# Row scatters of a routed expert layer: twelve in a row, or one at a time across the next step

## The chip, the cores and the metric

One core of one Trainium2 chip. The time is device microseconds for one execution of the whole kernel, median of three runs. All data is float32 except three small bf16 tiles.

## The reference

A transformer block with adaptive layer norm, for 8 images of 256 tokens and 256 channels:

```
mod = silu(c) @ wmod                       # 6 rows of 256 per image: sa, ca, ga, sb, cb, gb
h = layernorm(x) * (1 + ca) + sa
x = x + ga * attention(h)                  # 16 heads, ternary weights, chunks of 128 tokens with a carried state
h = layernorm(x) * (1 + cb) + sb
scores = sigmoid(h @ gate_w); best 4 of 8 groups, then best 6 of 64 experts
x = x + gb * (sum of 6 experts(h) + shared expert(h))
```

Each expert takes at most 48 tokens; the kernel keeps a table `rows_dram` with 64 slots for each of the 64 experts.

## The kernel before, in words

The kernel has three stages. **Token stage:** one step per image, `step(s, ...)` for s = 0 to 9 on every engine. Step s works on image s in attention (`cur`), on image s-1 in the output projection, residual and second norm (`has_prev`), and on image s-2 in the router's choice and the shared expert (`has_two`). **Expert stage:** 32 pairs of experts, `pair_step`; the token rows come back from DRAM (`rows_dram`), pass through the two experts and are scattered to `y_dram` by `put` (L489), one scatter a pair. **Last stage:** 16 tiles are read back, summed over their six experts (L1019), gated and stored.

Each engine has its own hand-written order of work in a step; counters (semaphores, `S[...]`) tie them together. `token_steps` (L257) calls the step for s = 0, 1, 2 as straight code, steps 3 to 6 as two turns of a hardware loop of two steps, and steps 7, 8, 9 as straight code again.

What the change and the prediction touch, in the order of one step:

- GpSimd's step (L454). `power` of `rstd1` for image s+1 (L456), `power` of `fac` for image s-1 (L458), `q_lam` (L463), `power` of `rstd2` for image s-1 (L465); then `h2s` (L469) and `h2row` (L473), the second norm's scale and shift; last `dispatch` (L441) of image s-2, twice six indirect DMAs (L449). Each writes 128 rows of `h2row` (336 floats) to the rows of `rows_dram` that `slot_ix` names.
- `h2row` and `slot_ix` have two buffers. GpSimd waits at L472 until the scatters of two images ago are written before it overwrites `h2row`.
- VectorE's step (L939): router scores of s-2 (L824), statistics of the first norm, shared expert, `out_norms` (L785: the row L790 waits for TensorE's L1120), `rms`, router choice (L840), mask 0 (L821), `state`, residual (L799, L805, L810) with the second norm's statistics (L654 to L662, whose last is `ve2`), first norm's output, second norm's output `z2` (L668), mask 1, `slots` (L919), which ends with `slot_ix`, and `shared_out`.
- TensorE's step (L1215): `project_qkv` (L1078 and on), scores, `project_out`, `values`, `norm2_transpose` (L1174, waits for `h2row`), logits (L1184), `norm1_transpose`, `gate_up` (L1193), and at the next step's head `out_stats` (L1120).
- ScalarE copies what TensorE leaves in PSUM: `qT`, `k_eo`, `v_eo`, `h2T`, `oT`, `r_exp`, `hT`, and `s_exp` (L614) after `gate_up`. `norm1_out` (L558) takes its scale and bias from `mod_cur`, which VectorE copies per image (L679).
- SyncE's queue loads `xa`, `mod_b` and `xres` in each step, and after the last step waits (L343) until all 96 row scatters are written; then it loads the rows for the experts (L346).

Of the kernel before, what the change touches and what calls it, by code (L numbers as in the profile page):

```python
# [5 lines left out]
ALU = mybir.AluOpType  # L6
# [7 lines left out]
P = 128  # L14
# [23 lines left out]
NBUF = 2  # L38
EPS_F = 1.1920928955078125e-07
# [23 lines left out]
def adaln_attention_moe(nc, x, qkv_w, qkv_norm_w, proj_w, proj_norm_w, norm_w, s, gate_w, bias,  # L63
                        w_gate, w_up, w_down, ws_gate, ws_up, ws_down, c, wmod, out):
    with ExitStack() as ctx:
# [58 lines left out]
        mod_cur = [sb(f"mod_cur{i}", [P, 4]) for i in range(2)]  # L124
# [22 lines left out]
        attn = sb("attn", [P, NT, C])  # L147
# [7 lines left out]
        h2row = [sb(f"h2row{i}", [P, NT, ROWW]) for i in range(2)]  # L155
# [24 lines left out]
        slot_ix = [sb(f"slot_ix{i}", [P, NT, 8], U32) for i in range(2)]  # L180
# [10 lines left out]
        wcol = [sb(f"wcol{i}", [P, 1]) for i in range(WBUF)]  # L191
        larger = sb("larger", [P, 8])
        rank = sb("rank", [P, 1])
        y_row = [sb(f"y_row{i}", [P, 1], U32) for i in range(WBUF)]

        spare = scm[:].rearrange("p r j q t -> p (r j q t)")
        row_bufs = [h[:] for h in h2row] + [spare[:, NT * ROWW * i:NT * ROWW * (i + 1)].rearrange("p (n c) -> p n c", n=NT)
                            for i in range(XBUF // 2 - 2)]
        xr = [row_bufs[i // 2][:, i % 2] for i in range(XBUF)]
        xt = [attn[:, i].rearrange("p (k r) -> p k r", k=KC) for i in range(NBUF)]  # L200
# [32 lines left out]
        ld_y2 ld_y3 ld_xr0 ld_xr1 ld_xr2 ld_xr3 st_mod st_zero st_rows0 st_rows1 st_put0 st_put1  # L233
        st_put2 st_put3 st_y0 st_y1 c_zero c_fill c_shape c_neg c_decay0 c_decay c_lam c_misc q_abs
        q_all q_tern q_tp q_sc q_w m_exp m_silu m_tp m_ct m_mm m_cols m_rows0 m_rows ln1_ve ln1_rstd
        z1_ready xt_done mod_cur_ready hT_ready hsq_ready q_done q_taken k_done k_taken v_done
# [20 lines left out]
        def token_steps(eng, step):  # L257

            for s in range(3):
                step(s, s % 2, s // 2, max(s - 1, 0) // 2)
            with eng.Fori(0, (B - 4) // 2) as i:
                step(2 * i + 3, 1, i + 1, i + 1)
                step(2 * i + 4, 0, i + 2, i + 1)
            step(B - 1, 1, (B - 1) // 2, (B - 2) // 2)
            step(B, 0, B // 2, (B - 1) // 2)
            step(B + 1, 1, (B + 1) // 2, B // 2)
# [26 lines left out]
        def _(sp):  # L295
# [44 lines left out]
            token_steps(sp, step)  # L340


            for par in range(2):  # L343
                sp.wait_ge(S[f"st_rows{par}"], 16 * B // 2 * NT * TOPK)
# [41 lines left out]
        def _(pool):  # L386
# [20 lines left out]
            for i in range(2):  # L407
                g.memset(h2row[i][:, :, TKEY:ROWW], 0.0)
# [32 lines left out]
            def dispatch(b, par, tile):  # L441

                if tile == 0:
                    pool.wait_ge(S["slots_ready"], b + 1)
                    pool.wait_ge(S["w_ready"], b + 1)
                    pool.wait_ge(S["h2_ready"], b + 1)
                    settle(par)
                for j in range(TOPK):
                    g.indirect_dma_start(  # L449
                        out=rows_dram, out_offset=bass.IndirectOffsetOnAxis(ap=slot_ix[par][:, tile, j:j + 1], axis=0),  # L450
                        in_=h2row[par][:, tile, :], in_offset=None, bounds_check=last_row,
                        oob_is_err=False).then_inc(S[f"st_rows{par}"], 16)

            def step(s, par, h, hp):  # L454
                if not at_end(s, B - 1):
                    power(rstd1[:], ve1[:], 0, "ln1_ve", "ln1_rstd", s + 2)  # L456
                if not before(s, 1) and not at_end(s, B + 1):
                    power(fac[:], fin[:, 4], 1, "f5", "f_ready", s)  # L458
                if not at_end(s, B):

                    pool.wait_ge(S["q_taken"], s + 1)
                    seen(pool, S["pv1"], s)
                    g.tensor_tensor(q_lam[:], qT[:, :, T:2 * T], lam_q[:], ALU.mult).then_inc(S["qlam_ready"], 1)  # L463
                if not before(s, 1) and not at_end(s, B + 1):
                    power(rstd2[:], ve2[:], 0, "ln2_ve", "ln2_rstd", s)  # L465

                    pool.wait_ge(S["z2_ready"], s)
                    pool.wait_ge(S[f"ld_modb{1 - par}"], 16 * (hp + 1))
                    g.tensor_tensor(h2s[:], z2[:], spread(mod_b[1 - par][:, 2], 1, NT), ALU.mult).then_inc(S["h2_mul"], 1)  # L469
                    pool.wait_ge(S["h2_mul"], s)  # L470
                    seen(pool, S["h2t_done"], s - 2)
                    seen(pool, S[f"st_rows{1 - par}"], 16 * NT * TOPK * hp)  # L472
                    g.tensor_tensor(h2row[1 - par][:, :, 0:C], h2s[:], spread(mod_b[1 - par][:, 1], 1, NT),  # L473
                                    ALU.add).then_inc(S["h2_ready"], 1)
                if not before(s, 2):
                    for tile in range(NT):
                        dispatch(s - 2, par, tile)
# [5 lines left out]
            token_steps(pool, step)  # L483
# [49 lines left out]
        def _(act):  # L533
# [24 lines left out]
            def norm1_out(b, par):  # L558

                act.wait_ge(S["xt_done"], b + 1)  # L560
                act.wait_ge(S["mod_cur_ready"], b + 1)
                seen(act, S["v_done"], b)
                seen(act, S["kt_done"], b)
                for j in range(KC):
                    last = a.activation(hT[:, j], ps_a[:, N * j:N * j + N], ACT.Identity,
                                        scale=mod_cur[par][:, 2 + j:3 + j], bias=mod_cur[par][:, j:j + 1])
                last.then_inc(S["hT_ready"], 1)
                for j in range(KC):
                    last = a.activation(hsq[:, j], ps_a[:, N * j:N * j + N], ACT.Square,  # L569
                                        scale=mod_cur[par][:, 2 + j:3 + j], bias=mod_cur[par][:, j:j + 1])  # L570
                last.then_inc(S["hsq_ready"], 1)

            def step(s, par, h, hp):
# [35 lines left out]
                if not at_end(s, B - 1):  # L609
                    norm1_out(s + 1, 1 - par)  # L610
# [5 lines left out]
            norm1_out(0, 0)  # L616
            act.wait_ge(S["c_misc"], 1)
            act.wait_ge(S["c_fill"], 1)
            token_steps(act, step)
# [24 lines left out]
        def _(dve):  # L644
# [30 lines left out]
            def norm1_apply(b, par):  # L675
                seen(dve, S["xt_done"], b)
                norm_apply(b, xa, mv1, rstd1, z1, "ln1", "z1_ready")
                seen(dve, S["hsq_ready"], b - 1)
# [629 lines left out]
```

## Time and profile before

| | us |
|---|---|
| runs | 515.25, 516.87, 517.76 (median 516.87) |
| span of the profiled execution, first to last instruction | 517.1 |
| GpSimd busy / VectorE busy / TensorE matmul busy in the span | 212.8 / 283.7 / 309.6 |
| first row scatter starts / last row scatter starts | 119.8 / 371.7 |

The profiled execution lies inside the range of the runs, 0.2 us from their median. A page of the profile gives the busy time of each engine, the chain of work that ended last, and the costliest groups. A timeline gives single instructions: start, duration, engine, line, operation, output and input, and in brackets how long the engine had been idle and what released it. "remote" is a release that the profile can't put down to an instruction of this core, "issue" an idle time that ended with no wait that it shows. A table by window gives busy time and granted clock in stretches of the span. A "q" after an engine's name stands for its queue of DMA issues and waits.

### The profile page before, as it was taken

To read this page: it belongs to the slowest core of one execution; us is meant where nothing else is said; L and a number is where in the kernel's file an instruction comes from. 1 tells how busy PE (TensorE), PEld (TensorE's weight loads), DVE (VectorE), ACT (ScalarE), POOL (GpSimd) and SP (SyncE) were. 2 spreads that over 40 slices of the span, in tenths; PEclk is the share of its full clock that TensorE was granted. 3 is DMA by queue.
4 is the path that set the end of the run, shared out by engine and by line. 5 is a ranking of instruction groups with operands and counts; after the bars stand their busy time and mean duration, and the time that the engine had idled before them with its cause. 6 is when DMAs were issued, how large, how long until landed. Compare 5 with 4: busy or idle time off the path is not lost.

```text
span 517.1 us, 7330 instructions
## 1 busy us (share of the span) xinstructions
PE 309.6 (60%) x2282; PEld 222.4 (43%) x2282; DVE 283.7 (55%) x1066; ACT 98.9 (19%) x253; POOL 212.8 (41%) x310
## 2 busy tenths in 40 slices
PE   0735695968678768859657867150089889940000
PEld 0424484856556556747445655040045444520000
DVE  3550516395194394393393392664067544727995
ACT  1411131413112212303113201000024332430000
POOL 4200112117517527327327237186615433553664
PEclk9958568896786886796787787655579865985555
DMA  7955992963411311311301300000059999119992
GB/s 224 399 183 178 260 317 71 239 214 127 171 35 61 125 47 47 122 41 39 122 20 38 122 22 8 0 5 2 3 153 300 277 270 228 57 38 379 333 323 96
DMA packets 62332, 73.63 MB, mean 142 GB/s; under 512 B 9458, under 2 KB 56955, under 8 KB 62304
## 3 DMA queue, kind: packets, MB, share of 16 engines
q1 hardware_dynamic: 41456, 53.37, 35.2%
q10 hardware_dynamic: 14704, 15.24, 8.4%
q0 software_dynamic: 6144, 4.66, 3.1%
q8 instruction: 15, 0.25, 0.2%
q14 instruction: 13, 0.11, 0.1%
HBM read 48.39 MB, written 40.93 MB: 173 GB/s over the span
## 4 chain that ended last, share of the span: by engine, by line
issue 27%; PE 19%; DVE 16%; POOL 15%; DMA 10%; another core or an unknown queue 5%; ACT 3%; SPq 2%; DVEq 1%; ACTq 0%; POOLq 0%
POOL rows_dram L449 8%; PE ps_s L1268 5%; DVE z L1019 4%; DMA h2row<-rows_dram 2%; DVE scm L821 2%; DMA xa<-in_L_attn_x 2%; DMA scm<-rows_dram 2%; DMA egu<-y_dram 2%; POOL rstd L435 2%; PE ps_o L1166 2%; SPq L300 1%; PE ps_o L1281 1%; PE ps_a L1257 1%; PE ps_c L1281 1%
## 5 line engine op out<-in xcount | busy, mean ns | idle before, releaser
L449 POOL DMA_INDIRECT rows_dram<-h2row,slot_ix x96 | 94.3, 983 | 28.1 <-issue 28.1
L435 POOL TENSOR_TENSOR rstd<-ve,half_exp 128x2 f32<-128x2 f32 x15 | 11.2, 743 | 133.6 <-DVE ve L662 133.4
L1019 DVE TENSOR_REDUCE z<-egu 128x256 f32<-128x1536 f32 x16 | 42.7, 2746 | 10.8 <-DMA egu<-y_dram 10.8
L439 POOL TENSOR_TENSOR pool_pad<-half_exp 128x1 f32<-128x1 f32 x72 | 13.7, 191 | 68.4 <-ACT oT L545 17.0
L821 DVE TENSOR_TENSOR scm<-ps_s,decay 128x2048 f32<-128x2048 f32 x16 | 36.6, 2285 | 4.9 <-PE ps_s L1146 4.9
L1268 PE MATMUL ps_s<-egu,attn 128*64 128x192 f32 x256 | 33.7, 391 | 0.1
L1078 PE MATMUL ps_a<-hT,w_qkv 128*128 128x256 f32 x64 | 24.6, 551 | 11.9 <-ACT hsq L569 7.1
L1174 PE MATMUL ps_a<-ident,h2row 128*128 128x128 f32 x32 | 8.9, 435 | 36.7 <-POOL h2row L473 36.7
L1166 PE MATMUL ps_o<-scm,v_eo 128*32 128x128 f32 x512 | 26.8, 357 | 5.6 <-DVE scm L821 5.6
L827 DVE TENSOR_SCALAR r_den<-r_exp 128x128 f32<-128x128 f32 x8 | 1.8, 230 | 44.0 <-issue 35.0
L545 ACT ACTIVATE h2T<-ps_a 128x512 f32<-128x512 f32 x8 | 4.8, 597 | 105.5 <-PE ps_a L1174 105.5
L1078 PEld LDWEIGHTS ps_a<-hT,w_qkv 128*128 128x128 f32 x64 | 16.9, 278 | 15.7 <-issue 12.4
L1268 PEld LDWEIGHTS ps_s<-egu,attn 128*64 128x64 f32 x256 | 18.7, 158 | 7.7 <-issue 2.5
L1174 PEld LDWEIGHTS ps_a<-ident,h2row 128*128 128x128 f32 x32 | 5.7, 217 | 37.7 <-POOL h2row L473 37.7
L1129 PE MATMUL ps_c<-w_proj,oT 128*128 128x256 f32 x64 | 17.2, 415 | 7.4 <-issue 3.8
L1166 PEld LDWEIGHTS ps_o<-scm,v_eo 128*32 128x32 f32 x512 | 16.8, 138 | 11.1 <-issue 10.4
L1193 PE MATMUL ps_c<-h2T,ws_gu 128*96 128x256 f32 x64 | 21.4, 495 | 0.0
L625 ACT ACTIVATE z<-ps_s 128x96 f32<-128x96 f32 x32 | 8.0, 251 | 66.3 <-PE ps_s L1268 63.1
L1101 PE MATMUL ps_c<-w_qkv,hT 128*128 128x256 f32 x64 | 20.6, 480 | 0.0
L1146 PE MATMUL ps_s<-qT,k_eo 32*128 32x128 f32 x512 | 20.2, 297 | 0.0
L1257 PE MATMUL ps_a<-ident,h2row 128*128 128x128 f32 x16 | 4.6, 377 | 25.8 <-DMA h2row<-rows_dram 25.8
L494 POOL DMA_INDIRECT y_dram<-oT,y_row x16 | 15.9, 994 | 9.3 <-POOL pool_pad L439 5.1
(212 smaller groups left out, 725.3 us busy)
## 6 DMA issues: line engine op xcount, KB each, us to landing
y_dram<-y_zeros ACTq DMA_DIRECT2D x8, 1536.0 KB
egu<-y_dram SPq DMA_DIRECT2D x16, 768.0 KB, 5.9
egu<-in_L_ffn_w_gate SPq DMA_DIRECT2D x16, 384.0 KB, 6.7
egu<-in_L_ffn_w_up SPq DMA_DIRECT2D x16, 384.0 KB, 7.9
ed<-in_L_ffn_w_down SPq DMA_DIRECT2D x16, 384.0 KB, 9.7
rows_dram<-scm SPq DMA_DIRECT2D x1, 5376.0 KB, 15.8
mod_b<-mod_dram SPq DMA_DIRECT2D x8, 384.0 KB
h2row<-rows_dram SPq DMA_DIRECT2D x8, 336.0 KB
```

Source lines behind the costliest of these rows:

```text
L435: g.tensor_tensor(out_, in_, half_exp[:, which], ALU.pow).then_inc(S[done], 1)
L449: g.indirect_dma_start(out=rows_dram, out_offset=bass.IndirectOffsetOnAxis(ap=slot_ix[par][:, tile, j:j + 1], axis=0), in_=h2row[par][:, t ...
L494: g.indirect_dma_start(out=y_dram, out_offset=bass.IndirectOffsetOnAxis(ap=y_row[w][:, 0:1], axis=0), in_=e_out[n], in_offset=None, bounds ...
L821: v.tensor_tensor(scm[:].rearrange("p r j q t -> p (r j q t)"), ps_s[:].rearrange("p r n -> p (r n)"), decay[:].rearrange("p r j q t -> p ...
L1019: v.tensor_reduce(ysum[m % NT], y_in[m].rearrange("p (j c) -> p c j", c=C), AX_X, ALU.add).then_inc(S["y_sum"], 1)
L1078: last = mm.matmul(ps_a[:, N * j:N * j + N], w_qkv[:, k, P * j:P * j + P], hT[:, k], start=(k == 0), stop=(k == KC - 1))
L1101: last = mm.matmul(ps_c[:, C * i:C * i + C], hT[:, k, T * i:T * i + T], w_qkv[:, k, 2 * C:3 * C], start=(k == 0), stop=(k == KC - 1))
L1129: last = mm.matmul(ps_c[:, C * i:C * i + C], oT[:, i, k], w_proj[:, k], start=(k == 0), stop=(k == KC - 1))
L1146: last = mm.matmul(ps_s[:, r, col:col + T], k_eo[q][32 * r:32 * r + 32, j, ts], qT[32 * r:32 * r + 32, j, ts], start=True, stop=True)
L1166: last = mm.matmul(dst[32 * r:32 * r + 32], vq, scm[:, r, j, q], start=(q == 0 and not tile), stop=(q == 1), skip_group_check=True)
L1193: last = mm.matmul(ps_c[0:F, N * g_:N * g_ + N], ws_gu[:, k, g_], h2T[:, k], start=(k == 0), stop=(k == KC - 1))
L1268: last = mm.matmul(e_gups[n][rows].rearrange("p (g f) -> p g f", f=F), xt[n][:, k, rows], egu[:, slot // 2, :, 2 * (slot % 2) + half, k], ...
```

## The change

GpSimd's work is written out for s = 0 to 7 and for the tail, and on the other engines `token_steps` runs all ten steps as straight code. The twelve scatters of an image go out in step s for image s-3 instead of s-2, and no longer in a row at the end of GpSimd's step: each stands at a point of its own. Seven of them stand behind a new wait on another engine's event: `kt_done`, `v_done`, `sc0` and `mk0` ahead of `rstd2`, `h2t_done`, `pv1` and `lg_done` at the step's end. `h2row` and `slot_ix` get a third buffer, and the count of written rows a third semaphore. The `mod_cur` copy goes away (ScalarE reads `mod_cols` itself), and the residual is written to `x2` in place, without `attn`, to make room.

```
-            def dispatch(b, par, tile):
+            def dispatch(b, lo, hi):
 
-                if tile == 0:
+                if lo == 0:
                     pool.wait_ge(S["slots_ready"], b + 1)
                     pool.wait_ge(S["w_ready"], b + 1)
                     pool.wait_ge(S["h2_ready"], b + 1)
-                    settle(par)
-                for j in range(TOPK):
+                    settle(b % 2)
+                for n in range(lo, hi):
+                    tile, j = n // TOPK, n % TOPK
                     g.indirect_dma_start(
...
+            def norm2_rows(b):
+
+                pool.wait_ge(S["z2_ready"], b + 1)
+                pool.wait_ge(S[f"ld_modb{b % 2}"], 16 * (b // 2 + 1))
+                g.tensor_tensor(h2s[:], z2[:], spread(mod_b[b % 2][:, 2], 1, NT), ALU.mult).then_inc(S["h2_mul"], 1)
+                pool.wait_ge(S["h2_mul"], b + 1)
+                seen(pool, S["h2t_done"], b - 1)
+                seen(pool, S[f"st_rows{b % HBUF}"], 16 * NT * TOPK * (b // HBUF))
+                g.tensor_tensor(h2row[b % HBUF][:, :, 0:C], h2s[:], spread(mod_b[b % 2][:, 1], 1, NT),
+                                ALU.add).then_inc(S["h2_ready"], 1)
+
+            def step(s):
+
+                d = s - 3
+                late = d >= 0
+                if s < B - 1:
                     power(rstd1[:], ve1[:], 0, "ln1_ve", "ln1_rstd", s + 2)
+                if late:
+                    dispatch(d, 0, 1)
+                if s >= 1:
                     power(fac[:], fin[:, 4], 1, "f5", "f_ready", s)
+                if late:
+                    dispatch(d, 1, 2)
+                pool.wait_ge(S["q_taken"], s + 1)
+                seen(pool, S["pv1"], s)
+                g.tensor_tensor(q_lam[:], qT[:, :, T:2 * T], lam_q[:], ALU.mult).then_inc(S["qlam_ready"], 1)
+                if late:
+                    dispatch(d, 2, 3)
+                    pool.wait_ge(S["kt_done"], s + 1)
+                    dispatch(d, 3, 4)
+                    pool.wait_ge(S["v_done"], s + 1)
+                    dispatch(d, 4, 5)
+                    pool.wait_ge(S["sc0"], s + 1)
+                    dispatch(d, 5, 6)
+                    pool.wait_ge(S["mk0"], s + 1)
+                    dispatch(d, 6, 7)
+                if s >= 1:
                     power(rstd2[:], ve2[:], 0, "ln2_ve", "ln2_rstd", s)
+                    if late:
+                        dispatch(d, 7, 8)
+                    norm2_rows(s - 1)
+                if late:
+                    dispatch(d, 8, 9)
+                    pool.wait_ge(S["h2t_done"], s)
+                    dispatch(d, 9, 10)
+                    pool.wait_ge(S["pv1"], s + 1)
+                    dispatch(d, 10, 11)
+                    pool.wait_ge(S["lg_done"], s)
+                    dispatch(d, 11, 12)
...
-            token_steps(pool, step)
+            for s in range(B):
+                step(s)
+
+            power(fac[:], fin[:, 4], 1, "f5", "f_ready", B)
+            dispatch(B - 3, 0, 3)
+            power(rstd2[:], ve2[:], 0, "ln2_ve", "ln2_rstd", B)
+            dispatch(B - 3, 3, 4)
+            norm2_rows(B - 1)
+            dispatch(B - 3, 4, NT * TOPK)
+            dispatch(B - 2, 0, NT * TOPK)
+            dispatch(B - 1, 0, NT * TOPK)
```

## Rows read from the trace of the kernel before

**Rows 1.** The page: busy time of each engine, and the ending chain's shares by line

```profile
PE 309.6 (60%) x2282; PEld 222.4 (43%) x2282; DVE 283.7 (55%) x1066; ACT 98.9 (19%) x253; POOL 212.8 (41%) x310
...
POOL rows_dram L449 8%; PE ps_s L1268 5%; DVE z L1019 4%; DMA h2row<-rows_dram 2%; DVE scm L821 2%; DMA xa<-in_L_attn_x 2%; DMA scm<-rows_dram 2%; DMA egu<-y_dram 2%; POOL rstd L435 2%; PE ps_o L1166 2%; SPq L300 1%; PE ps_o L1281 1%; PE ps_a L1257 1%; PE ps_c L1281 1%
```

**Rows 2.** Windows between rstd2 starts: length, busy PE PEld DVE ACT POOL, clock, DMA

```profile
85.48:114.11 28.63, 21.93 (x216) 18.24 (x217) 18.49 (x84) 7.48 (x17) 5.40 (x6) 0.88 0.75 211
114.11:152.53 38.42, 28.86 (x224) 23.07 (x223) 21.43 (x95) 7.54 (x17) 17.71 (x19) 0.73 0.32 109
152.53:189.93 37.40, 28.01 (x224) 22.39 (x222) 21.59 (x95) 7.54 (x17) 17.37 (x20) 0.77 0.24 79
189.93:227.34 37.41, 27.81 (x223) 22.28 (x222) 21.32 (x95) 7.54 (x17) 17.40 (x19) 0.77 0.22 72
227.34:266.41 39.07, 27.85 (x224) 22.54 (x223) 21.56 (x95) 7.54 (x17) 17.38 (x20) 0.78 0.20 67
266.41:303.85 37.44, 27.30 (x221) 21.45 (x220) 20.18 (x88) 7.54 (x17) 16.69 (x18) 0.77 0.20 64
303.85:334.53 30.68, 12.94 (x85) 9.81 (x83) 16.29 (x79) 2.34 (x5) 15.88 (x17) 0.70 0.04 10
```

**Rows 3.** Timeline of step 4: its twelve scatters' first and last, gate_up and s_exp

```profile
195.71 1.06 POOL L449 DMA_INDIRECT rows_dram<-h2row,slot_ix  x1 [0.16 <-issue]
...
201.16 2.98 PE L1193 MATMUL ps_c<-h2T,ws_gu 128*96 128x256 f32 x8
...
209.85 0.97 POOL L449 DMA_INDIRECT rows_dram<-h2row,slot_ix  x1 [0.30 <-issue]
...
212.75 0.38 ACT L614 ACTIVATE s_exp<-ps_c 96x256 f32<-96x256 f32 x1 [5.16 <-remote]
```

**Rows 4.** Timeline of step 1, without scatters: the same two instructions

```profile
95.44 1.89 PE L1193 MATMUL ps_c<-h2T,ws_gu 128*96 128x256 f32 x8
...
97.45 0.38 ACT L614 ACTIVATE s_exp<-ps_c 96x256 f32<-96x256 f32 x1
```

**Rows 5.** Timeline of the expert stage: TensorE and ScalarE around one lone scatter

```profile
440.82 0.99 POOL L494 DMA_INDIRECT y_dram<-oT,y_row  x1 [0.48 <-POOL pool_pad L439]
440.91 0.65 PE L1281 MATMUL ps_o<-ed,s_h 96*64 96x256 f32 x4
...
441.61 0.47 ACT L545 ACTIVATE oT<-ps_o,wcol 128x256 f32<-128x256 f32 x1 [0.32 <-PE ps_o L1281]
...
442.89 0.99 POOL L494 DMA_INDIRECT y_dram<-oT,y_row  x1 [0.48 <-POOL pool_pad L439]
```

**Rows 6.** Timeline of step 2: GpSimd's rstd2 and h2s, VectorE's z2, slow gate_up

```profile
114.11 0.80 POOL L435 TENSOR_TENSOR rstd<-ve,half_exp 128x2 f32<-128x2 f32 x1 [11.81 <-DVE ve L662]
...
115.01 0.74 DVE L668 TENSOR_SCALAR z<-x,mv,rstd 128x256 f32<-128x256 f32 x2 [0.25 <-POOL rstd L435]
...
115.83 1.27 POOL L469 TENSOR_TENSOR h2s<-z,mod_b 128x512 f32<-128x512 f32 x1 [0.93 <-DVE z L668]
...
125.33 3.34 PE L1193 MATMUL ps_c<-h2T,ws_gu 128*96 128x256 f32 x8
```

**Rows 7.** Timeline of step 8: VectorE's out_norms starts late

```profile
326.42 0.16 DVE L790 SCALAR_TENSOR_TENSOR fin<-ps_o,a 128x2 f32<-128x2 f32 x1 [6.54 <-remote]
```

**Rows 8.** Timeline of the token stage's end: the last two bursts, first row load

```profile
339.31 1.06 POOL L449 DMA_INDIRECT rows_dram<-h2row,slot_ix  x1 [0.16 <-issue]
...
353.44 0.43 DVE L897 TENSOR_SCALAR h2row<-w_raw,w_rec 128x64 f32<-128x64 f32 x2
353.49 0.97 POOL L449 DMA_INDIRECT rows_dram<-h2row,slot_ix  x1 [0.30 <-issue]
...
357.66 0.99 POOL L449 DMA_INDIRECT rows_dram<-h2row,slot_ix  x1 [0.15 <-issue]
...
371.74 0.97 POOL L449 DMA_INDIRECT rows_dram<-h2row,slot_ix  x1 [0.30 <-issue]
373.91 0.88 SPq L346 DMA_DIRECT2D h2row<-rows_dram  x2
```

More of the change, by code:

```diff
@@ L38 @@
 NBUF = 2
+HBUF = 3
 EPS_F = 1.1920928955078125e-07
@@ L154, in adaln_attention_moe @@
         h2s = sb("h2s", [P, NT, C])
-        h2row = [sb(f"h2row{i}", [P, NT, ROWW]) for i in range(2)]
+        h2row = [sb(f"h2row{i}", [P, NT, ROWW]) for i in range(HBUF)]
         h2T = sb("h2T", [P, KC, N])
@@ L179, in adaln_attention_moe @@
         key = sb("key", [P, NT, E])
-        slot_ix = [sb(f"slot_ix{i}", [P, NT, 8], U32) for i in range(2)]
+        slot_ix = [sb(f"slot_ix{i}", [P, NT, 8], U32) for i in range(HBUF)]
         s_exp = sb("s_exp", [F, N])
@@ L255, in adaln_attention_moe, with token_steps @@
         y_v = y_dram.rearrange("(t p j) c -> t p (j c)", p=P, j=TOPK)
[L257 to L268, printed above, removed]
+        def token_steps(step, last):
+            for t in range(last + 1):
+                step(t, t % 2, t // 2, max(t - 1, 0) // 2)
         def pair_steps(eng, step):
@@ L338, in step @@
                 sp.dma_start(xres[:], x_t[s]).then_inc(S["ld_xres"], 16)
-            token_steps(sp, step)
-            for par in range(2):
-                sp.wait_ge(S[f"st_rows{par}"], 16 * B // 2 * NT * TOPK)
+            token_steps(step, B + 1)
+            for i in range(HBUF):
+                sp.wait_ge(S[f"st_rows{i}"], 16 * ((B - 1 - i) // HBUF + 1) * NT * TOPK)
             def load_rows(d, buf):
@@ L406, in _ @@
                    allow_small_or_imprecise_dtypes=True)
-            for i in range(2):
+            for i in range(HBUF):
                 g.memset(h2row[i][:, :, TKEY:ROWW], 0.0)
@@ L454, in step @@
-            def step(s, par, h, hp):
-                if not at_end(s, B - 1):
+                        out=rows_dram,
+                        out_offset=bass.IndirectOffsetOnAxis(ap=slot_ix[b % HBUF][:, tile, j:j + 1], axis=0),
+                        in_=h2row[b % HBUF][:, tile, :], in_offset=None, bounds_check=last_row,
+                        oob_is_err=False).then_inc(S[f"st_rows{b % HBUF}"], 16)
+            def norm2_rows(b):
[7 more added lines that the diff above has]
+                                ALU.add).then_inc(S["h2_ready"], 1)
@@ L464, in step @@
-                if not before(s, 1) and not at_end(s, B + 1):
-                    power(rstd2[:], ve2[:], 0, "ln2_ve", "ln2_rstd", s)
[L467 to L474, printed above, removed]
@@ L804, in residual @@
                 for i in range(NT):
-                    last = v.scalar_tensor_tensor(out=attn[:, i], in0=ps_c[:, C * i:C * i + C], scalar=fac[:, i:i + 1],
+                    last = v.scalar_tensor_tensor(out=x2[par][:, i], in0=ps_c[:, C * i:C * i + C], scalar=fac[:, i:i + 1],
                                                   in1=mod_b[par][:, 0], op0=ALU.mult, op1=ALU.mult)
@@ L896, in router_choice @@
                 for i in range(NT):
-                    last = v.tensor_scalar(h2row[par][:, i, C:KEYS], w_raw[:, i], w_rec[:, i:i + 1], ROUTE_SCALE,
+                    last = v.tensor_scalar(h2row[b % HBUF][:, i, C:KEYS], w_raw[:, i], w_rec[:, i:i + 1], ROUTE_SCALE,
                                            ALU.mult, ALU.mult)
@@ L968, in step @@
                 if has_two:
-                    slots(s - 2, par)
+                    slots(s - 2)
                     shared_out(s - 2, par)
@@ L975, in _ @@
             dve.wait_ge(S["st_zero"], 16)
-            token_steps(dve, step)
+            token_steps(step, B + 1)
             def pair_step(q, i, m):
@@ L1173, in norm2_transpose @@
                     for i in range(NT):
[L1174 removed]
+                        last = mm.transpose(ps_a[:, N * j + T * i:N * j + T * i + T], h2row[b % HBUF][:, i, P * j:P * j + P],
                                            ident[:])
@@ L1242, in step @@
                     gate_up(s - 1)
-            token_steps(pe, step)
+            token_steps(step, B + 1)
             pe.wait_ge(S["pre_ready"], B)
```

71 lines of the change are left out of this document (29 added, 42 removed).

## Prediction

> **What bounds the kernel now.** I read the page first. No engine is near its limit: GpSimd is busy for 212.8 of 517.1 us, VectorE for 283.7, TensorE for 309.6, and of the chain that ended last the row scatters at L449 are the largest single line, 8% [rows 1]. A chain spread over so many lines means a step in which the engines hand work to each other, so I took the windows next, cut at each start of `rstd2`. That instruction stands on every step's path: behind it come `z2`, `h2s`, `h2row`, the transposes and everything after them. The first window holds no scatter and lasts 28.63 us. The next five hold twelve each and last 38.42, 37.40, 37.41, 39.07 and 37.44, together 189.74 us; step 8, without attention, still takes 30.68 [rows 2]. GpSimd itself is busy for only 17.4 of 37.4 us, so its work fills less than half of a step, and still the twelve scatters cost about 8.8 us (37.4 - 28.6), or 0.73 us each.
>
> The timeline of a step shows how. The twelve run back to back from 195.71 to 210.82, one every 1.28 us (14.14 us over 11 spacings). Meanwhile TensorE's last `gate_up` matmul ends at 204.14, but ScalarE, idle for 5.16 us, starts the `s_exp` that waits for it only at 212.75, 8.6 us later and 1.9 us after the last scatter [rows 3]. Without scatters the same pair is 0.12 us apart (95.44 + 1.89 to 97.45) [rows 4]. So a burst holds up events of other engines, and the hold outlasts the burst. Twelve scatters from 195.71 until release at 212.75 are 17.0 us, or 1.42 us each, as if each took 1.42 us of something that is fed every 1.28. What it is the trace doesn't say. In the expert stage, though, one scatter every 2.07 us (440.82, 442.89) holds up nobody: TensorE's L1281 ends at 441.56, in the middle of one, and ScalarE starts at 441.61 [rows 5]. The spacing decides, then, and the change alters the spacing.
>
> **The change, part by part.** I follow the start of `rstd2` from step to step.
>
> *The first window with a gain.* Steps 1 and 2 stay as they are up to `rstd2` at 114.11. Before, image 0's burst came right behind it; now the first scatter comes in step 3. So all five windows to the old 303.85 lose their burst. The base of each is 28.63 us [rows 2].
>
> *TensorE's clock.* The scatter-free window had a granted clock of 0.88, the others 0.73 to 0.78 [rows 2]. `gate_up` shows both levels: 1.89 us for eight matmuls at 95.44 [rows 4], 3.34 at 125.33, at about half [rows 6], a stretch not yet held up by much. If `gate_up` is slow, this instruction alone adds 1.45 us and the logits and transposes near it about as much by estimate, 2.7 in all. I take half of the steps as slow: +1.35 us a step. Bounds: 0 and 2.7.
>
> *The scatter behind `rstd2`.* The power ends at 114.91, `h2s` starts at 115.83, because it waits for `z2` [rows 6]. A scatter with its gap takes 1.28, so it ends at 116.2 and `h2s` starts some 0.2 later: +0.6 us a step, on the path. That is the one scatter that GpSimd's own path feels.
>
> *The other eleven.* On GpSimd they find room: 17.4 us busy of 31. Behind them stand `fac`, `q_lam`, `rstd2` and the next `rstd1`. The waits on `kt_done`, `v_done`, `sc0` and `mk0` stand ahead of `rstd2`, but all four events come before VectorE's residual, which makes `rstd2`'s input; the mask behind `mk0` is followed by the residual and its statistics, longer than one scatter. `lg_done` stands ahead of the next `rstd1`, whose input VectorE makes only behind the router scores, which wait for the same logits. So no new wait ends last, and nobody waits long for what is queued behind it. What the eleven do to others' events has a lower bound of 0 [rows 5] and an upper of the burst's 0.73 each, 8 us a step. Their spacing is between the two: scatters three to six follow events that come within 5 us or so and will nearly touch; the rest have 2 us or more. Since it is nearest to the expert stage, I take +0.6 us a step.
>
> *Unrolled steps and small edits.* Straight steps (38.42 for the window into step 3, 37.44 into step 7) and looped ones (37.40, 37.41, 39.07) take the same [rows 2]: 0, with bounds -1.6 (the odd 39.07) and +1 a step. The dropped `mod_cur` copy, the residual in place and the third buffer: 0. The copy runs while VectorE waits for `rstd2`, the residual writes the same bytes, and a buffer's scatters now end a whole step before GpSimd's wait at its reuse. SyncE's queue waits on the same events as before; DMA is 20 to 32% busy in these windows, so 12 scatters in other places meet nothing new.
>
> A step is then 28.63 + 1.35 + 0.6 + 0.6 = **31.2 us**. Five are 156.0 instead of 189.74: -33.7. `rstd2` of step 7 starts at 270.1.
>
> *Step 8.* Before, VectorE's `out_norms` sat idle for 6.54 us until 326.42 in the wake of a burst [rows 7]; for the other late events of that burst I take 1.2 more, an estimate a little below the 1.42 of one scatter. 30.68 - 6.54 - 1.2 + 0.6 = 23.6 us. -7.1. `rstd2` of step 8 starts at 293.7.
>
> *What is left for the end.* Here the change pays. Image 5's last eight scatters, image 6's and image 7's twelve each, 32, now all come behind the last `h2row`. Before, from `rstd2` of step 8 (334.53) to the first scatter of the burst there it was 4.78 us (339.31), then came 24, with a gap at 354.46 to 357.66 in which GpSimd waited for the last slots; the last ended at 372.71 [rows 8]. Now: 4.78 + 0.6 + 32 x 1.277 = 40.9, and 0.7 for two settling instructions: 47.0 instead of 38.2, +8.8. The wait for the last slots is covered: they came 18.4 us behind the first scatter (339.31 to 357.7), and the 20 ahead of image 7's take 25.5. From the last scatter's end to the loads it was 1.2 us (372.71 to 373.91) [rows 8]; I keep that. If the backlog of 0.14 to 0.23 us a scatter also holds up the last writes, the end comes up to 7 us later.
>
> Expert and last stage start cold as before, from the same event, 0.
>
> Sum: -33.7 - 7.1 + 8.8 = -32.0. 517.1 - 32.0 = 485.1 for the profiled execution, which stands 0.2 above the median: **485 us**.
>
> **A rule against it.** Row 353.49 shows a scatter that starts while VectorE runs a `tensor_scalar` out of and into SBUF; it takes 0.97 us, as all do [rows 8]. VectorE's `z2`, 0.74 us, is such an instruction, and the moved scatter will stand right beside it [rows 6]. The Trainium skill, "SBUF — State Buffer", section "A bandwidth-pool intuition that's wrong (but worth ruling out)" and the box above it, says that GpSimd cannot write descriptors while VectorE holds the shared port in a two-port mode, which fp32 `tensor_scalar` can enter. By that rule the scatter would end behind `z2`.
>
> **The rivals.**
>
> *Slower: a lone scatter holds up as much as one in a burst.* Each of the 12 points stands right behind an event, where the next engine starts, and a step is one chain of such handovers. If each costs it 0.73 us or more, a step is 28.6 + 8.8 + 0.6 = 38, and nothing is won there. The tail's +8.8 then stays, and step 8 gains 4: 5 x 38 = 190, +0.3; together +5. With each scatter at 0.85 and a backlog of 5 in the tail it is +17; I put this case between the two, at 528. It decides from a step of 37.6 us on (372.71 - 114.11 - 23.6 - 47.0 = 188.0, over 5), so 0.75 us a scatter. For it: the hold of 1.42 each [rows 3]. Against: [rows 5].
>
> *Partly given back.* Scatters three to six bunch up, TensorE idles and its clock stays low (+2.7 instead of 1.35), others' events come 1.5 late: a step of 34. 5 x 34 = 170, step 8 at 25, tail 47 + 5: the end is at 361, or 505 us.
>
> *Better.* Base step of 28.6 + 0.6, no more: -43.6 in five steps, the rest as above: 475.
>
> *The scatter waits for `z2`.* Then `h2s` starts some 0.74 us later in each of six steps: 4.4 us, 489.5. Row 353.49 speaks against it, though that instruction is short.
>
> *It does not do what it says:* the waited events are long past, the scatters run in bunches of six, and tail and gain cancel: 516.
>
> **How the numbers follow.** Chances: forecast 0.50, partly given back 0.18, better 0.12, slower 0.10, the scatter waits for `z2` 0.07, no effect 0.03. Faster, 0.87, holds all but two; a measurement of this kernel can tell about 0.5%, 2.6 us, from no change. The range leaves out the slower case, the last one, and the far ends of the others: 470 (a step of 28.6 and no other cost) to 508.
>
> **What would show it.** Windows between starts of `rstd2` of 30 to 32.5 us in steps 3 to 7; `s_exp` less than 1.5 us behind `gate_up`'s end; a scatter in each of twelve places, still 0.97 long; `h2s` 1.5 us behind the power instead of 0.9; 32 scatters in a row at the end, 41 us long, TensorE idle below them; last scatter near 340. Windows over 34, or row scatters that outlast 350, would make the prediction wrong.

## The result and the profile after

The changed kernel takes 491.65 us (median of four runs, 484.59 to 497.92), the kernel before 517.32 on the same chip (515.25 to 521.20). The ratio is 0.939, with a 95% interval of 0.927 to 0.952; it and all ratios below compare only the faster executions of both kernels, so they differ a little from those of the medians (here 0.950), and the profiled execution is not among the faster ones. The forecast was 485 us, with a range of 470 to 508. The profiled execution took 493.44 us, with a span of 491.7: it lies 1.8 us above the median, where that of before lay 0.2 from its own.

The page: busy time, and the shares of the chain that ended last.

```profile
PE 293.6 (60%) x2282; PEld 211.4 (43%) x2282; DVE 285.3 (58%) x1058; ACT 99.1 (20%) x253; POOL 214.5 (44%) x311
...
DMA out<-z 5%; POOL rows_dram L444 5%; PE ps_s L1297 4%; DMA scm<-rows_dram 4%; PE ps_o L1195 4%; DMA h2row<-rows_dram 3%; DVE scm L850 3%; PE ps_b L1213 3%; DMA xa<-in_L_attn_x 2%; POOL h2s L454 2%; POOL h2row L458 2%; PE ps_o L1191 2%; PE ps_a L1203 2%; SPq L294 2%; POOL rstd L429 1%
```

GpSimd does the same work (214.5 us, before 212.8 [rows 1]); the scatters, now L444, fall from 8% of the chain to 5%. TensorE's busy time falls by 16 us without one matmul less: the granted clock of the five windows from 113.38 to 268.27 below is 0.83 or 0.84, where the same five had 0.73 to 0.78 [rows 2].

The windows between starts of `rstd2`, as [rows 2]: length, busy PE, PEld, DVE, ACT and POOL, granted clock, DMA share, GB/s.

```profile
84.78:113.38 28.60, 21.89 (x216) 18.21 (x217) 18.43 (x83) 7.43 (x17) 5.40 (x6) 0.88 0.74 213
113.38:144.72 31.34, 24.84 (x221) 20.44 (x220) 21.20 (x94) 7.63 (x17) 12.89 (x14) 0.84 0.35 119
144.72:176.05 31.33, 24.35 (x221) 20.17 (x220) 21.54 (x94) 7.63 (x17) 17.76 (x19) 0.84 0.31 105
176.05:205.75 29.70, 22.43 (x206) 18.66 (x207) 21.75 (x94) 7.51 (x17) 17.85 (x20) 0.83 0.28 93
205.75:237.19 31.44, 26.02 (x244) 21.49 (x237) 21.45 (x94) 7.63 (x17) 17.62 (x20) 0.83 0.26 85
237.19:268.27 31.08, 24.24 (x222) 20.12 (x220) 20.47 (x87) 7.63 (x17) 16.97 (x19) 0.84 0.23 76
268.27:291.31 23.04, 13.24 (x86) 10.09 (x83) 16.59 (x79) 2.34 (x5) 12.05 (x13) 0.78 0.05 14
```

Five windows took 189.7 us and now take 154.9; step 8 takes 23.0 instead of 30.7. The order of a step, from the timeline (step 3 from `rstd2` on):

```profile
144.72 0.82 POOL L429 TENSOR_TENSOR rstd<-ve,half_exp 128x2 f32<-128x2 f32 x1 [1.96 <-DVE ve L693]
145.65 0.74 DVE L699 TENSOR_SCALAR z<-x,mv,rstd 128x256 f32<-128x256 f32 x2 [0.36 <-POOL rstd L429]
145.74 1.04 POOL L444 DMA_INDIRECT rows_dram<-h2row,slot_ix  x1 [0.20 <-issue]
146.80 1.28 POOL L454 TENSOR_TENSOR h2s<-z,mod_b 128x512 f32<-128x512 f32 x1
...
155.95 0.97 POOL L444 DMA_INDIRECT rows_dram<-h2row,slot_ix  x1 [0.90 <-PE ps_b L1213]
...
156.32 2.79 PE L1222 MATMUL ps_c<-h2T,ws_gu 128*96 128x256 f32 x8
159.14 0.38 ACT L644 ACTIVATE s_exp<-ps_c 96x256 f32<-96x256 f32 x1 [0.65 <-PE ps_c L1222]
```

`s_exp` starts 0.03 us behind the end of `gate_up` (156.32 + 2.79), where it stood 8.6 us behind it in step 4 of [rows 3]. `h2s` waits for the scatter and starts 1.26 us behind the power's end; in [rows 6] it was 0.92.

The end of the token stage, GpSimd and VectorE:

```profile
296.10 1.01 POOL L444 DMA_INDIRECT rows_dram<-h2row,slot_ix  x1 [0.15 <-issue]
...
319.53 0.29 DVE L957 TENSOR_TENSOR key<-keep,row_key 128x128 f32<-128x128 f32 x1 [3.96 <-remote]
...
323.79 0.17 DVE L964 COPY h2row<-token_key 128x2 f32<-128x2 f32 x1 [2.46 <-remote]
323.86 0.17 DVE L965 TENSOR_SCALAR slot_ix<-h2row 128x16 uint32<-128x16 f32 x1
...
324.54 0.19 POOL L433 TENSOR_TENSOR pool_pad<-half_exp 128x1 f32<-128x1 f32 x1 [3.12 <-DVE slot_ix L965]
```

Here is the old stall again, "remote" waits of VectorE under a run of twenty scatters. They make the last `slot_ix` late, and GpSimd itself now waits 3.12 us for it. The last scatter starts at 339.29.

From there to the end of the span there were 144.4 us before (517.1 - 372.71) and are 151.4 now (491.7 - 340.26). So the token stage gave 32.4 us and 7.0 came back in the two stages behind it. The change leaves their order of work as it was, but not all of their tiles: the experts' `xt` lies in `x2` instead of `attn`, and the single `wcol` and `y_row` tiles are now columns of one tile each. On the chip of group 2 below the same stretch went from 143.6 to 149.8 us.

### The profile page after: what moved, and what is told of

Its sections match the earlier page's. It is cut to its first block, busy times and chain, and to the rows that moved or that the text cites. A ratio compares the mean times of both kernels' runs of the same rounds, so it can differ in the third digit from the quotient of the medians.

```text
span 491.7 us, 7103 instructions
## 1 busy us (share of the span) xinstructions
PE 293.6 (60%) x2282; PEld 211.4 (43%) x2282; DVE 285.3 (58%) x1058; ACT 99.1 (20%) x253; POOL 214.5 (44%) x311
## 4 chain that ended last, share of the span: by engine, by line
PE 23%; issue 20%; DMA 18%; DVE 17%; POOL 14%; ACT 2%; SPq 2%; another core or an unknown queue 1%; POOLq 0%; DVEq 0%; ACTq 0%
DMA out<-z 5%; POOL rows_dram L444 5%; PE ps_s L1297 4%; DMA scm<-rows_dram 4%; PE ps_o L1195 4%; DMA h2row<-rows_dram 3%; DVE scm L850 3%; PE ps_b L1213 3%; DMA xa<-in_L_attn_x 2%; POOL h2s L454 2%; POOL h2row L458 2%; PE ps_o L1191 2%; PE ps_a L1203 2%; SPq L294 2%; POOL rstd L429 1%
## 5 line engine op out<-in xcount | busy, mean ns | idle before, releaser
L444 POOL DMA_INDIRECT rows_dram<-h2row,slot_ix x96 | 95.6, 996 | 51.8 <-issue 17.5
L1297 PE MATMUL ps_s<-egu,x 128*64 128x192 f32 x256 | 34.2, 395 | 0.1
L1286 PE MATMUL ps_a<-ident,h2row 128*128 128x128 f32 x16 | 5.0, 407 | 31.3 <-DMA h2row<-rows_dram 31.3
L1013 DVE COPY x<-ps_a 128x256 f32<-128x256 f32 x16 | 6.7, 419 | 27.6 <-PE ps_a L1286 27.4
L1297 PEld LDWEIGHTS ps_s<-egu,x 128*64 128x64 f32 x256 | 18.9, 159 | 8.1 <-issue 3.2
L1107 PE MATMUL ps_a<-hT,w_qkv 128*128 128x256 f32 x64 | 19.3, 455 | 3.1 <-DVE mod_rows L779 3.0
L525 POOL DMA_INDIRECT y_dram<-oT,y_rows x16 | 15.9, 994 | 9.3 <-POOL pool_pad L433 5.6
L1018 DVE SCALAR_TENSOR_TENSOR z<-z,ps_s 128x96 f32<-128x96 f32 x32 | 8.1, 253 | 20.0 <-ACT z L656 11.1
L1175 PEld LDWEIGHTS ps_s<-qT,k_eo 32*128 32x128 f32 x512 | 17.3, 201 | 4.6 <-issue 4.6
```

What stands on the lines that cost most here:

```text
L444: g.indirect_dma_start(out=rows_dram, out_offset=bass.IndirectOffsetOnAxis(ap=slot_ix[b % HBUF][:, tile, j:j + 1], axis=0), in_=h2row[b % ...
L525: g.indirect_dma_start(out=y_dram, out_offset=bass.IndirectOffsetOnAxis(ap=y_row[w][:, 0:1], axis=0), in_=e_out[n], in_offset=None, bounds ...
L1107: last = mm.matmul(ps_a[:, N * j:N * j + N], w_qkv[:, k, P * j:P * j + P], hT[:, k], start=(k == 0), stop=(k == KC - 1))
L1175: last = mm.matmul(ps_s[:, r, col:col + T], k_eo[q][32 * r:32 * r + 32, j, ts], qT[32 * r:32 * r + 32, j, ts], start=True, stop=True)
L1297: last = mm.matmul(e_gups[n][rows].rearrange("p (g f) -> p g f", f=F), xt[n][:, k, rows], egu[:, slot // 2, :, 2 * (slot % 2) + half, k], ...
```

## The experiments

The four groups ran on four chips, and this turned out to matter: the kernel before took 476.4, 518.5, 478.5 and 521.7 us on them.

**1. One part at a time.** First the burst kept where it was, in the straight-line code of the changed kernel (its other edits kept):

```
-                if late:
-                    dispatch(d, 0, 1)
...
-                if late:
-                    dispatch(d, 8, 9)
-                    pool.wait_ge(S["h2t_done"], s)
...
+                if s >= 2:
+                    dispatch(s - 2, 0, NT * TOPK)
```

> The changed kernel with its straight steps, three buffers and without mod_cur and attn, but the twelve scatters of image s-2 in a row at the end of GpSimd's step, as before. Theory (the spacing of the scatters is what pays): windows between rstd2 starts go back to 37 to 39 us, the time to about 517. Rival (straight code and the small edits pay): windows stay near 31, the time near 490.

Then the burst one step later, as `dispatch(s - 3, 0, 12)` at the end of the step:

> The changed kernel with all twelve scatters of image s-3 in a row at the end of step s: one step later, but not singly. Theory: the window into step 3 loses its burst (about 29), the four behind it are at 37 to 38, step 8 at 30 and the tail's 32 scatters stay: 29 + 4 x 37.4 + 30.5 from 113.4 on, 323 at rstd2 of step 8, last scatter near 371, time about 516 to 522. Rival (what pays is that the scatters wait for nothing, since they are a step late): near 490.

Then the changed kernel without the seven waits, its scatters at the same places in GpSimd's order:

> The changed kernel without the seven new waits; the scatters keep their places in GpSimd's order. Scatters three to seven then run back to back, as do nine to twelve. Theory (hold grows with a bunch, 0.14 us or more a scatter): a step of 32 to 34 us, 5 to 12 us over the changed kernel, about 500. Rival A (order alone pays, the waits only cost): same as the changed kernel or up to 3 us less. Rival B (a scatter must stand behind an event): near 517.

And the kernel before, with two tiny instructions behind every scatter:

```
+PADS = 2
...
+                    for k in range(PADS):
+                        g.tensor_tensor(fill[:, at:at + 1], half_exp[:, 0, 0:1], half_exp[:, 0, 0:1], ALU.add)
```

> The kernel before, looped and with the burst in its old place, but with two tiny GpSimd instructions behind each row scatter, so that the twelve start some 1.65 us apart instead of 1.28. GpSimd's work grows by 12 x 0.4 = 4.5 us a step. Theory (a scatter takes 1.42 us of something that others' events share; fed slower than that, nothing piles up): events are no longer late by more than 1 us, windows fall from 37.4 to 30 to 33, the end of the token stage gives 9 us back, time about 495. Rival (each scatter costs a fixed 0.73 wherever it stands, or GpSimd's own time is what counts): windows of 37.4 or 4 us more, time 517 to 550.

Measured: 480.93 for the burst in place (1.003 of before, 0.996 to 1.009), 492.00 for the later burst (1.028, 1.019 to 1.036), 487.24 without waits (1.026, 1.018 to 1.034), 485.62 for the spaced burst. None is faster than the kernel before, which took 476.42 there, and the three theories that expected a burst to be held up (37 us a window, about 517 us in all; 500 without waits) are missed. Timeline of the burst in place:

```profile
181.76 1.06 POOL L444 DMA_INDIRECT rows_dram<-h2row,slot_ix  x1 [0.16 <-issue]
...
186.25 1.89 PE L1195 MATMUL ps_c<-h2T,ws_gu 128*96 128x256 f32 x8
...
188.26 0.38 ACT L617 ACTIVATE s_exp<-ps_c 96x256 f32<-96x256 f32 x1
...
195.91 0.97 POOL L444 DMA_INDIRECT rows_dram<-h2row,slot_ix  x1 [0.30 <-issue]
```

The twelve are 1.286 us apart on the mean, as in [rows 3], and hold up nobody: `s_exp` starts 0.12 us behind the matmul. Its windows are 31.75, 31.43, 29.58, 31.67, 30.99 and 24.44. So on this chip a burst has no hold. The time of the kernel before there agrees, though no profile shows it: the burst in place, its windows put into the sum of before, gives 34.3 (189.7 - 155.4) + 6.2 us less, and the kernel before is 40.9 us faster here than on the first chip. Without the waits the changed kernel's windows are 30.65, 29.36, 31.69, 31.35 and 29.10, 30.4 on the mean. The changed kernel itself was not run there; elsewhere it has 31.0, with one short window in five instead of two, so the waits cost next to nothing. Whether they are needed where a burst is held, no run shows. What is left on such a chip is the price: the later order leaves 32 scatters for the end.

**2. The same question where the kernel before is slow.** The kernel before itself, the changed kernel itself, the spaced burst again, and a new split: four of an image's scatters go out at the end of the step that the kernel before used for all twelve, eight in the next, and none stands between `rstd2` and `h2s`; 26 are left for the end.

```
+                if s >= 2:
+                    dispatch(s - 2, 0, 1)
+                    pool.wait_ge(S["h2t_done"], s)
+                    dispatch(s - 2, 1, 2)
+                    pool.wait_ge(S["pv1"], s + 1)
+                    dispatch(s - 2, 2, 3)
+                    pool.wait_ge(S["lg_done"], s)
+                    dispatch(s - 2, 3, 4)
```

> The kernel before, unchanged, once more with its trace: the first four runs were on a chip where it took 476 and not 517 us. Theory now (the hold of others' events by a burst differs from chip to chip): where it takes some 517 us, windows between rstd2 starts are 37 us and s_exp starts 5 to 9 us behind gate_up; where it takes some 476, windows are 30 to 32 us and s_exp starts within 1 us. Rival (the chips differ in memory or clock speed, all over the kernel): the 40 us are spread over all stages.

> The changed kernel, unchanged, beside the kernel before on the same chip. Theory: its windows are 30 to 31.5 us on any chip, and its last row scatter ends near 340. On a chip where bursts hold up events it is 25 to 32 us faster than before; on one where they don't, nothing is won in the steps and the longer tail costs 9 to 13 us, so some 2% slower (485 to 490 against 476). Rival (the change gains by itself, wherever it runs): 25 us faster in both cases.

> A version that might beat both: an image's first four scatters go out at the end of its own step, behind the new slots, the other eight at the points of the next step; none stands between rstd2 and h2s; 26 scatters are left behind the last h2row instead of 32. Theory: windows 0.5 us shorter than the changed kernel's (30 to 31), 6 scatters less at the end (-7.7 us) unless the last slots come later than the 14 scatters ahead of them: 6 to 11 us under the changed kernel on any chip. Rival (the first four, close behind the slots and others' events, hold up the logits): windows 1 to 2 us longer, no gain.

> The kernel before with two tiny GpSimd instructions behind each row scatter (one every 1.53 us instead of 1.28), as in the spaced run before. Theory: on a chip where bursts hold up events, the hold vanishes or falls below 1 us and the windows are those of the quick chip (30 to 32), about 20 us faster than before in all; on one where they don't, 9 us slower (36 more gaps of 0.25 us in the tail, the rest hidden). Rival (the hold is a fixed cost per scatter): as slow as before on either chip, plus the added time.

Measured: 515.77 for before itself (1.002, 0.996 to 1.008), 488.26 for the changed kernel (0.946, 0.932 to 0.961), 485.71 for the split (0.949, 0.939 to 0.959), 486.42 for the spaced burst (0.947, 0.936 to 0.959). The kernel before, step 4, in the timeline:

```profile
193.43 1.06 POOL L449 DMA_INDIRECT rows_dram<-h2row,slot_ix  x1 [0.16 <-issue]
...
198.88 3.14 PE L1193 MATMUL ps_c<-h2T,ws_gu 128*96 128x256 f32 x8
...
207.57 0.97 POOL L449 DMA_INDIRECT rows_dram<-h2row,slot_ix  x1 [0.30 <-issue]
210.42 0.38 ACT L614 ACTIVATE s_exp<-ps_c 96x256 f32<-96x256 f32 x1 [6.53 <-remote]
```

and the spaced burst on the same chip:

```profile
213.70 1.06 POOL L451 DMA_INDIRECT rows_dram<-h2row,slot_ix  x1 [0.16 <-issue]
215.29 0.99 POOL L451 DMA_INDIRECT rows_dram<-h2row,slot_ix  x1 [0.16 <-issue]
...
217.83 1.89 PE L1198 MATMUL ps_c<-h2T,ws_gu 128*96 128x256 f32 x8
...
219.84 0.38 ACT L619 ACTIVATE s_exp<-ps_c 96x256 f32<-96x256 f32 x1
...
230.75 0.99 POOL L451 DMA_INDIRECT rows_dram<-h2row,slot_ix  x1 [0.16 <-issue]
```

This is the decisive pair. Everything is as before but the two tiny instructions and, with them, the distance of two scatters: 1.29 us in the first, 1.55 in the second (17.05 over 11, with `pool_pad` in it). At 1.29 `s_exp` comes 8.4 us behind its matmul (8.4 to 11.4 us in steps 3 to 6), at 1.55 0.12 us behind it; the second timeline is of step 5, and in step 4 it is 0.04 us. Its idle time from 113 to 305 us, grouped by line, first before, then spaced:

```profile
L614 ACT ACTIVATE s_exp<-ps_c 96x256 f32<-96x256 f32 x5 | 1.9, 379 | 28.4 <-remote 26.0 <-PE ps_c L1193 2.4
```

```profile
L619 ACT ACTIVATE s_exp<-ps_c 96x256 f32<-96x256 f32 x6 | 2.3, 378 | 4.3 <-PE ps_c L1198 4.3
```

So spacing, with no new order and no new wait, gives the change's whole gain on this chip: 486.4 against 488.3. Whether it is the distance that counts, or that an instruction stands between, this pair can't tell. In the changed kernel on this chip some scatters follow another with nothing but a wait between them, 1.9 to 3.5 us apart, and `s_exp` is 0.03 to 0.13 us behind its matmul, which speaks for the distance but doesn't settle it. Up to three stand 1.3 us apart there (165.51, 166.82, 168.10), and their window is still 31.35 us long, so such a short run costs nothing that shows.

The split was expected 6 to 11 us below the changed kernel and is 2.6 below it. Its last scatter does start 8.0 us sooner (328.5 against 336.5), but its expert stage takes 96.5 us against 94.1.

**3. What is left of the time after.** The expert stage, from the last row scatter to the last `y_dram` scatter, took 89.9 us before and 94.6 after. I suspected where the tiles lie: the third buffers had moved `egu`. So these kernels declare them behind `ed` (and `wcols` in the 32 bytes where `mod_cur` was), and the first of them is otherwise the changed kernel:

```
-        h2row = [sb(f"h2row{i}", [P, NT, ROWW]) for i in range(HBUF)]
+        h2row = [sb(f"h2row{i}", [P, NT, ROWW]) for i in range(2)]
...
         ed = sb("ed", [F, QUADS, 4, C])
+        h2row.append(sb("h2row2", [P, NT, ROWW]))
```

> The changed kernel with its tiles put back to where the kernel before has them, modulo 512 bytes: the third h2row and slot_ix are declared after ed, and the merged wcols tile takes the 32 bytes where mod_cur was, so that scm, h2row0, h2row1, egu and ed (all that the transfers of the expert and the last stage write) start at the same offset of a 512-byte line as before. Nothing else is changed. The expert stage, from the last row scatter to the last y_dram scatter, took 94.6 and 94.1 us in two profiles of the changed kernel, and 89.9 and 89.0 in two of the kernel before; the transfers moved 227 to 239 GB/s in the slice 35 to 40 us behind the last row scatter, against 262 and 283. Theory placement (the tiles' offsets slow the transfers): the stage takes 89 to 91 us here and the slice moves over 255 GB/s; total 4 to 5 us under the changed kernel's. Rival clock (the stage's length goes with how long TensorE's granted clock stays at half speed while the transfers starve it, and that is set by when the work arrives, not where it lies): the stage takes 93 to 97 us again with a mean granted clock under 0.81 over the 90 us from 5 us behind the last row scatter, and the total is the changed kernel's within 2 us. Step windows stay 31 us under both.

The split, with the same placement:

> The split of an image's scatters (four in its own step, eight in the next, 26 left for the end) with the same placement of the tiles as in the other kernel of this call. Split without it took 485.7 us on one chip: last row scatter at 328.5, expert stage 96.5. Theory placement: 89 to 91 us for the stage, about 479 in all on a chip like that one. Rival clock: 94 to 97 us again, total 485 (on such a chip).

And the price of spread scatters in a step:

> The changed kernel with the row scatters of the first five images left out (steps 3 to 7 issue none, and the waits among them are gone too); the last three images' scatters stay as they are. It tells what twelve spread scatters cost a step. The prediction's sum (28.63 for a step without scatters, 1.35 for the clock, 0.6 + 0.6 for the scatters): rstd2 to rstd2 takes 30.0 us in steps 3 to 7, 1.2 less than with the scatters. Rival (spread scatters still hold the other engines, each by 0.1 us or more): under 29.5. Rival (they cost nothing at all): 30.8 to 31.2, as now. The end, behind step 8, is unchanged under all of them: 47 to 49 us from rstd2 of the last image to the last row scatter.

Measured, where the kernel before took 478.54: 486.50 (1.030, 1.021 to 1.038), 477.93 (1.011, 1.003 to 1.020) and 484.67. The expert stages were 93.6, 88.1 and 91.5 us: the first speaks against the placement, the second for it. The rival in the clock is not borne out as it stands either: 93.6 us came with a mean clock of 0.82 and not under 0.81, and `before` took 89.9 at the same 0.82. The windows of the kernel without scatters:

```profile
111.78:142.89 31.11, 24.64 (x221) 20.32 (x220) 21.08 (x94) 7.63 (x17) 5.45 (x7) 0.84 0.25 82
142.89:173.79 30.90, 24.46 (x221) 20.20 (x220) 21.02 (x94) 7.63 (x17) 5.44 (x6) 0.83 0.23 82
173.79:204.61 30.82, 24.36 (x221) 20.15 (x220) 21.04 (x94) 7.64 (x17) 5.44 (x6) 0.83 0.24 82
204.61:235.45 30.84, 24.32 (x221) 20.11 (x220) 21.10 (x94) 7.64 (x17) 5.44 (x6) 0.83 0.24 82
```

and two of the changed kernel's (with the tiles moved) on the same chip:

```profile
174.91:206.25 31.34, 24.07 (x221) 19.96 (x220) 21.80 (x94) 7.63 (x17) 17.88 (x20) 0.84 0.28 89
206.25:235.40 29.15, 22.14 (x221) 18.37 (x220) 21.53 (x94) 7.42 (x17) 17.89 (x20) 0.88 0.29 92
```

A step without one scatter takes 30.9 us; with twelve spread ones it is 31.3 to 31.5 in four windows, and 29.15 in the one whose granted clock is 0.88.

**4. The split once more.**

> The split of an image's scatters with the tiles' placement of before, once more, on whatever chip comes. Theory (the hold is a property of the chip, and a burst at 1.28 us a scatter meets it while single ones don't): where the kernel before takes about 517 us, this one takes 474 to 484, a ratio of 0.92 to 0.94, better than the changed kernel's 0.939 to 0.946; where the kernel before takes about 477 us, this one is level with it, 0.995 to 1.015, as it was on the last chip. Rival (placement or chance in the expert stage decides): the expert stage, 88.1 us in its first profile, comes out at 94 us or more, and the total at 484 or more on either kind of chip.

It came to a chip on which the kernel before takes 521.7 us: 481.15 us, ratio 0.926 (0.919 to 0.932). The ratio is the best of all, but the changed kernel did not run beside it, and on the chip of group 3 the split is 1.1% slower than the kernel before. Bursts are held up on this chip too: in the row of scatters at the end VectorE has a "remote" wait again and GpSimd waits 3.0 us for the last slots, and the same kernel in group 3 shows neither:

```profile
312.77 0.29 DVE L959 TENSOR_TENSOR key<-keep,row_key 128x128 f32<-128x128 f32 x1 [1.93 <-remote]
...
314.89 0.19 POOL L435 TENSOR_TENSOR pool_pad<-half_exp 128x1 f32<-128x1 f32 x1 [2.97 <-DVE slot_ix L967]
```

The windows are 31.16, 30.93, 30.85, 30.85 and 30.74, within 0.05 of those without any scatter on the chip of group 3; on that chip itself the split's are 0.14 us longer on the mean (31.01 against 30.88). Spread, and with none ahead of `h2s`, twelve scatters cost a step next to nothing. But its expert stage took 94.6 us, not 88.1, so placement does not decide. This is one kernel in two executions, on two chips, and the clock differs. The 90 us of the expert stage from 5 us behind the last row scatter, first the execution of 88.1 us, then that of 94.6:

```profile
332.40:422.40 90.00, 74.30 (x480) 39.12 (x480) 50.54 (x257) 31.25 (x96) 37.87 (x64) 0.86 0.72 196
```

```profile
334.30:424.30 90.00, 81.35 (x480) 41.17 (x480) 50.78 (x256) 31.44 (x96) 37.27 (x64) 0.78 0.70 182
```

and the two ends among the others, the spaced burst of group 1 (stage 88.4) and the burst in place (97.5):

```profile
340.90:430.90 90.00, 69.31 (x480) 37.64 (x480) 50.35 (x256) 31.02 (x96) 37.83 (x64) 0.92 0.73 195
```

```profile
332.10:422.10 90.00, 86.42 (x480) 42.50 (x480) 50.78 (x256) 30.68 (x95) 34.58 (x60) 0.72 0.69 181
```

The same 480 matmuls are busy for 69 to 86 us. In the burst in place the clock is at 0.50 to 0.55, the lower of its two levels (1.2 GHz), from 362.1 to 407.1, and TensorE is busy for 43.4 of these 45 us; in the spaced burst it is at 1.00 from 345.9 to 395.9. The stage's length goes with the clock, but not only with it: at a mean of 0.82 it is 89.9 us (before), 91.5 (without scatters) and 93.6 (tiles moved), at 0.78 it is 92.0 (spaced burst of group 2) and 94.1 (changed kernel, same chip).

## Why the prediction was right, point by point

From the old span to the new, forecast and measured: five windows -33.7 and -34.9, step 8 -7.1 and -7.6, the end of the token stage +8.8 and +10.8, the two stages behind it 0 and +7.0; 0.7 us are gained ahead of the first window. The sum is -32.0 against -25.4.

**The mechanism held, where it exists.** The reading was that a burst at 1.28 us a scatter holds other engines' events and that spacing decides. The spaced burst of group 2 shows it by itself. The estimate of 1.42 us for what a scatter takes lies between the two spacings measured, 1.29 with the hold and 1.55 without. What the prediction could not see in one trace: the hold belongs to some chips. It was there on the first, where the forecast was to be met, and on those of groups 2 and 4. On that of group 1 the burst in place showed none, and there was nothing to win in the steps; the changed kernel itself never ran on such a chip, only its version with moved tiles, 3% slower than the kernel before. So the forecast holds for the kind of chip whose trace it was read from, and no reason in it could have told the other kind apart.

**The step of 31.2.** Measured 31.0 on the mean, but two of its terms were off, with opposite signs. Base and clock, 28.63 + 1.35 = 30.0, should have been 30.5. "I take half of the steps as slow" is what failed: four of five are. A step without scatters and slow takes 30.9; `gate_up` takes 2.79 us in the step shown, and 1.89, its time at the higher clock, only in the short window, 29.70. In group 3 the one window at 0.88 is 2.2 to 2.3 us shorter than its neighbours, so the bound of 2.7 was near. The base itself was right, though VectorE executes 83 instructions in it and 94 in the next window: 29.15 at the same clock of 0.88, less 0.5 for the scatters, is 28.65. The scatters, 0.6 + 0.6, should have been 0.5 (31.4 in the slow windows of group 3 against 30.9): the one behind `rstd2` costs 0.34 (1.26 against 0.92), and the other eleven next to nothing. The unrolled steps, the waits and the third buffer were priced at 0. The no-waits run bears out the waits, and the burst in place, with straight code and three buffers, is level with the kernel before (1.003), though its longer stages behind may hide something; neither edit was tried alone.

**Step 8**: 23.0 against 23.6. **The end of the tokens**: 340.3 against 340.7, by two errors that cancel again: `rstd2` of step 8 came 2.4 us sooner than forecast, and the rest took 2.0 longer. "The wait for the last slots is covered" was wrong in the first trace. The last slots took 27.8 us from the first scatter (296.10 to 323.86) instead of 18.4, because twenty scatters in a row ahead of them held VectorE up; GpSimd waited 3.1 us. On the chip of group 2 they were covered by 4 us (the last slots at 318.2, GpSimd ready at 322.1), on that of group 3, without holds, by 12 (308.3, 320.3). The sum of 47.0 from `rstd2` to the last scatter's end was 49.0 with the wait, 45.6 to 45.8 in the other profiles of this order.

**"Expert and last stage start cold as before, from the same event, 0"** is the step that cost the 6.6 us between the forecast of 485.1 and the span of 491.7. It was +7.0: 4.7 in the expert stage, 2.3 in the last. Over fourteen profiles the expert stage took 88.1 to 97.9 us, with a clock of 0.92 to 0.72, so half of this can be one execution's luck. Not all: four profiles with the old token stage average 89.8 us and ten with the new straight-line one 94.5. The granted clock of the stage goes with part of it; why it is lower there, and where the 2 to 4 us at an equal clock come from, stays open. That the placement of the third buffers decides is refuted. All ten also have `xt` in `x2` and the merged `wcol` and `y_row` tiles, and that was not tried. The last stage, from the last `y_dram` scatter on, took 55.4 to 55.6 us in the four and 56.4 to 57.8 in the ten; that is open too.

**The rivals.** Slower, because a lone scatter holds as much as one in a burst: refuted; the split's twelve cost 0.14 us a step in all on the chip of group 3. The scatter that waits for `z2`: the one at 145.74 ran beside `z2` (145.65 to 146.39) and took 1.04 us, as the other first ones behind an instruction of GpSimd's own do, and `h2s` started 1.26 us behind the power, sooner than the 1.5 forecast without that rule. So the rule that the prediction took from the Trainium skill ("SBUF — State Buffer", section "A bandwidth-pool intuition that's wrong (but worth ruling out)" and the box above it) is not seen here. Nor is it refuted: one `z2` instruction takes 0.41 us, no less than the statistics over the same 128x256 (`bn`, L685, 0.41), so no row shows that `z2` was in a two-port mode. The better case needed a clock that never falls. The case in which part is given back was right in its sign and wrong in its place: not in the steps but behind them. The case without any effect, bunches of six, is not what happened.

## What to carry to other kernels

Before work is moved across a whole step, stretch the burst: where bursts are held up, two instructions of 0.2 us between indirect DMAs gave the gain of a rewrite (where they aren't, neither gained). Price the clock by the steps that you want to shorten, not by the quick one that serves as the base: four of five ran slow. And measure on more than one chip: the same edit was 6% faster on one and, with its tiles moved, 3% slower on another.

## What the runs showed of the chip beyond this

Chips differ by 8 to 10% on one program, 476 and 478 against 517 to 522 us, and it isn't the engines: single instructions take the same (0.97 us a scatter, 1.89 us for `gate_up` at the higher clock on both). By the bursts of groups 1 and 2 it is whether back-to-back indirect scatters hold up others' events; what in the chip makes it so no run shows. And the expert stage of one kernel took 88.1 us at a mean granted clock of 0.86 and 94.6 at 0.78, on two chips; what lowers the clock there is not shown.
